# Second cross-attention of a two-layer Perceiver: scores of two key tiles, then weighted values of two key tiles

## What is computed

```python
kv = (mem @ W_kv).reshape(B, Nkv, 2, HEADS, HEAD_DIM)          # mem: (32, 1601, 256)
k = kv[:, :, 0].transpose(0, 2, 1, 3); v = kv[:, :, 1].transpose(0, 2, 1, 3)
q = (x @ W_q).reshape(B, Nq, HEADS, HEAD_DIM).transpose(0, 2, 1, 3)
attn = softmax(jnp.einsum('bhqd,bhkd->bhqk', q, k) * SCALE, axis=-1)
out = jnp.einsum('bhqk,bhkd->bhqd', attn, v).transpose(0, 2, 1, 3).reshape(B, Nq, C)
return out @ W_proj + b_proj
```

## Time and profile before

| | us |
|---|---|
| median of 3 runs | 3062.28 |
| lowest, highest | 3057.97, 3067.33 |
| profiled execution | 3058.96 |
| its span, first to last instruction | 3057.2 |
| TensorE busy in the span | 2627.0 |
| VectorE, ScalarE, GpSimd busy | 1533.6, 1410.0, 931.4 |

### The profile page before, as it was taken

How to read it: one execution, slowest core, us unless ns; L and a number is a source line. 1 busy time by engine, 2 the same in 40 slices (tenths; PEclk the granted TensorE clock), 3 DMA queues, 4 the chain that set the end, 5 groups by cost and what they waited for, 6 DMA issues and landing times.

```text
span 3057.2 us, 75335 instructions
## 1 busy us (share of the span) xinstructions
PE 2627.0 (86%) x31984; PEld 2205.9 (72%) x31988; DVE 1533.6 (50%) x2629; ACT 1410.0 (46%) x2563; POOL 931.4 (30%) x867
## 2 busy tenths in 40 slices
PE   6999732239999999999999999999999974699997
PEld 3555411138888888888888888888888753699997
DVE  3444377724445355454454454454454434477775
ACT  1221111124655655655655655655656521365564
POOL 1000034243432442442443443443443302211121
PEclk9999955569999999999999999999999975799999
DMA  8888500031110100100100100101101002466664
GB/s 340 317 319 316 212 0 0 0 119 34 35 34 23 37 31 23 45 23 23 45 23 23 45 23 29 40 23 34 34 23 34 2 1 90 156 209 202 217 200 150
DMA packets 48580, 270.17 MB, mean 88 GB/s; under 512 B 4896, under 2 KB 23584, under 8 KB 33696
## 3 DMA queue, kind: packets, MB, share of 16 engines
q1 hardware_dynamic: 40160, 255.82, 22.9%
q0 software_dynamic: 8160, 10.29, 2.2%
HBM read 247.58 MB, written 20.61 MB: 88 GB/s over the span
## 4 chain that ended last, share of the span: by engine, by line
issue 38%; PE 28%; POOL 21%; DVE 6%; DMA 3%; ACT 2%; POOLq 1%; SPq 0%; DVEq 0%; ACTq 0%
POOL k_lo L530 7%; POOL ctx_lo L538 6%; PE PS L1025 3%; PE PS L1005 3%; PE PS L1355 2%; PE PS L1356 2%; PE PS L1357 2%; POOL sideB L558 2%; POOL qbd_lo L543 2%; PE PS L1277 1%; DMA unit_raw<-in_experts 1%; PE PS L1372 1%; PE PS L1373 1%; PE PS L1374 1%; POOL slots_d L633 1%
## 5 line engine op out<-in xcount | busy, mean ns | idle before, releaser
L1624 DVE TENSOR_REDUCE mpart<-PS 128x1 f32<-128x802 f32 (+1 forms) x512 | 487.6, 987 | 464.4 <-PE PS L1141 464.4
L825 ACT ACTIVATE probs<-PS 128x1024 f32<-128x1024 f32 (+1 forms) x416 | 425.6, 1024 | 252.7 <-PE PS L1277 247.0
L530 POOL TENSOR_TENSOR k_lo<-sideB,k_hi 128x400 fp32r<-128x400 f32 (+1 forms) x256 | 255.7, 999 | 376.3 <-ACT k_hi L761 375.9
L538 POOL TENSOR_TENSOR ctx_lo<-ctx_raw,ctx_hi 128x801 fp32r<-128x801 f32 x128 | 224.6, 1764 | 459.2 <-ACT ctx_hi L773 459.2
L1277 PE MATMUL PS<-qbd_hi,k_hi 64*128 64x256 f32 (+1 forms) x1664 | 312.6, 372 | 0.0
L1141 PE MATMUL PS<-k_hi,qbd_hi 128*128 128x512 f32 (+2 forms) x1024 | 262.3, 358 | 23.1 <-POOL ctx_lo L538 13.6
L1153 PE MATMUL PS<-probs,vals 128*32 128x64 f32 x13312 | 272.9, 222 | 3.3 <-ACT probs L825 2.9
L1153 PEld LDWEIGHTS PS<-probs,vals 128*32 128x32 f32 x13312 | 205.3, 110 | 66.8 <-issue 11.0
L760 ACT COPY sideB<-PS 128x400 f32<-128x400 f32 (+1 forms) x256 | 126.6, 494 | 274.7 <-PE PS L1121 274.7
L1128 PE MATMUL PS<-wkv_hi,ctx_hi 128*128 128x256 f32 (+1 forms) x832 | 236.4, 284 | 0.0
L1277 PE MATMUL PS<-qbd_hi,k_lo 64*128 64x256 f32 (+1 forms) x1664 | 234.4, 278 | 0.1
(11 more groups left out here) (319 smaller groups left out, 6220.6 us busy)
## 6 DMA issues: line engine op xcount, KB each, us to landing
unit_raw<-in_experts SPq DMA_DIRECT2D x46, 1536.0 KB, 7.1
ctxN<-in_ctxN SPq DMA_DIRECT2D x16, 3328.0 KB, 10.8
ctxT<-in_ctxT SPq DMA_DIRECT2D x16, 3204.0 KB, 10.5
ctx_raw<-in_ctxT SPq DMA_DIRECT2D x64, 801.0 KB, 4.4
slots_d<-pad_rows SPq DMA_DIRECT2D x2, 2990.0 KB, 18.5
xg<-slots_d SPq DMA_DIRECT2D x23, 260.0 KB, 2.8
x<-in_x SPq DMA_DIRECT2D x1, 2048.0 KB, 10.0
sum_d<-x SPq DMA_DIRECT2D x1, 2048.0 KB, 6.3
```

The costliest lines, as they stand in the source:

```text
L530: g.tensor_tensor(k_lo[:, n, a, c:c + width], k_raw[p % 2][:, 0:width], k_hi[:, n, a, c:c + width].bitcast(F32), ALU.subtract).then_inc(s. ...
L538: g.tensor_tensor(ctx_lo[:, a, cols], ctx_raw[:, cols], ctx_hi[:, a, cols].bitcast(F32), ALU.subtract).then_inc(s.ctx_lo_ready, 1)
L825: act.activation(probs[rows, t % PROBS, :], PS[rows, 1024 * (t % 2):1024 * (t % 2) + 1024], ACT.Exp).then_inc(s.pr_ready, 1)
L1624: v.tensor_reduce(mpart[:, pair, half:half + 1], PS[:, at:at + width], AX, ALU.max).then_inc(s.mx_red, 1)
```

## The change

The score loop of `pe_batch` runs over pairs of key tiles. For an even t it issues the scores of t and t + 1, then finish and prepare of t, then the weighted values of t - 2 and t - 1, then finish and prepare of t + 1. Key tile 12 stands alone in its pair. Since the two weigh calls come later, each key tile's scores now wait for themselves until ScalarE has read the banks that they overwrite, that is for the exponentials of t - 2. `probs` gets a fourth buffer. Room for it comes from three places: `inv_sb` is gone (the reciprocal is written to its place in `attn4`, and multiplied there), `attn4` becomes part of `sideB`, and `attn_ch` moves behind the area that the stages share. The programs of ScalarE, VectorE and GpSimd keep their order.

```diff
-PROBS = 3
+PROBS = 4
...
-        inv_sb = sb_b("inv", [P, D])
-        attn4 = sb_b("attn4", [P, 4, P])
...
+        attn4 = sideB[:, 1792:2304].rearrange("p (g t) -> p g t", g=4)
...
-                for t in range(KEY_TILES):
+                def scores(t):
                     rows = slice(0, keys_of(t))
                     keys = slice(t * P, t * P + keys_of(t))
                     halves = [(r, slice(64 * r, 64 * r + 64)) for r in range(2)]
+                    if t >= 2:
+                        pe.wait_ge(s.pr_ready, exps_before + t - 1)
...
                     mm.then_inc(s.sc_ps, 1)
-                    if t >= 1:
-                        weigh(n, t - 1)
+
+                def beside(t):
                     if not first:
                         finish(n * KEY_TILES + t)
                     if not last:
                         prepare(n * KEY_TILES + t)
+
+                exps_before = T["pr"].now()
+                for t in range(0, KEY_TILES, 2):
+                    for one in range(t, min(t + 2, KEY_TILES)):
+                        scores(one)
+                    beside(t)
+                    if t:
+                        weigh(n, t - 2)
+                        weigh(n, t - 1)
+                    if t + 1 < KEY_TILES:
+                        beside(t + 1)
...
-                v.reciprocal(inv_sb[:, :], bank(7, D)).then_inc(s.vec_step, 1)
-                v.wait_ge(s.vec_step, own())
-                v.tensor_tensor(attn4[:, :, b * S:b * S + S], sums_sb[:, :].rearrange("p (g q) -> p g q", g=4),
-                                inv_sb[:, :].rearrange("p (g q) -> p g q", g=4), ALU.mult).then_inc(s.attn_ready, 1)
+                mine = attn4[:, :, b * S:b * S + S]
+                v.reciprocal(mine, bank(7, D).rearrange("p (g q) -> p g q", g=4)).then_inc(s.vec_step, 1)
+                v.wait_ge(s.vec_step, own())
+                v.tensor_tensor(mine, sums_sb[:, :].rearrange("p (g q) -> p g q", g=4), mine, ALU.mult).then_inc(s.attn_ready, 1)
```

More of the change, by code:

```diff
@@ L146, in build @@
         cat = sb("cat", [P, D])
-        attn_ch = sb("attn_ch", [P, KT, P])
         shift = sb("shift", [P, HEADS * S // 2], BF16)
@@ L221, in build @@
         hq_buf = sb("hq_buf", [P, 2048])
+        attn_ch = sb("attn_ch", [P, KT, P])
         identb = sb("identb", [P, P], BF16)
```

## The result

The changed kernel took 3081.62 us (median of 4 runs, 3080.72 to 3087.41) against 3060.34 us for the kernel before in the same comparison. The ratio is 1.007, with a 95% interval of 1.0048 to 1.0091: **slower by about 21 us**. The forecast was 3032 us, faster, and its range ended at 3052. The profiled execution of after has a span of 3079.8 us, that of before 3057.2.

The account below looks back on a forecast made before the run. TensorE was taken to bound stage B. Joints -42.2, step 2 wait +18.8, step 4 -5.3, GpSimd ahead +1.7 and first pair +0.5 gave -26.5 us from 3058.96: 3032 us forecast, range 3016 to 3052.

Parts of the forecast that it names:

- The joints: Stage B, TensorE: joining same-shape groups saves 0.09 us per score pair and 0.13 per weighted-values pair, -42.2 us in all.
- The rivals in which the joints give nothing or only half: Stage B: joints worth nothing, 3072 us, chance 0.07; only weighted values join, 3050 us, chance 0.13 including partial joints.
- The wait at step 2: TensorE's transposes wait 1.34 us for the normalised tile in 15 pairs, +18.8 us, bounds 0 and 20.
- The same instructions of the same size: Fourth buffer, moved tiles and reciprocal written in place cost nothing, on VectorE while TensorE projects.
- the paragraph on ScalarE: Exponentials cause no wait in plain key tiles; only the first pair, without finish steps, meets ScalarE, +0.5 us.
- The clock: Rival: granted clock falls after step 2's wait, three key tiles at half clock, 54 us, 3085 us; chance 0.04.
- Step 4: TensorE's wait for spread keys falls from 0.62 to about 0.3 us, -5.3 us over 15 pairs, bounds 0 and -8.
- GpSimd ahead of the next batch (n = 1): Before the next batch's first maxima, the 0.13 us wait stays or grows by up to 0.1; +1.7 us taken.
- The first pair: Without finish steps, its scores start back to back and meet ScalarE and its rounding: +0.5 us.

Follow-up runs that it names:

- the runs with 1.27 and 1.56: Changed kernel, GpSimd's first context subtraction held until the normalised tile is written: 3039.65 us; kernel before, context rounded one key tile earlier: 3080.63 us.
- the kernel with single tiles and GpSimd's wait: Changed kernel with old order for key tiles 0 to 3 where n = 0, and GpSimd's first context subtraction held until the normalised tile: 3027.99 us.
- the kernel in which GpSimd waits: Changed kernel, but GpSimd begins its first context subtraction in a pair only when VectorE has written the normalised tile: 3039.65 us, ratio 0.9933.
- the kernel of single tiles: Changed kernel with old order for key tiles 0 to 3 where n = 0 and finish steps exist, pairs from tile 4: 3033.52 us, ratio 0.9911.

## Why the prediction was wrong, step by step

**The joints: right.** Forecast 0.09 us per joined score pair and 0.13 per joined weighted values. Measured 0.09 (0.12 instead of 0.21 at the joint) and 0.15 (1.03 instead of 1.18). With n = 1, where nothing disturbs it, the part with scores fell from 25.31 to 23.93 us, 1.38 us for six joints of each kind; the forecast was 6 x 0.22 = 1.32. The rivals in which the joints give nothing or only half are refuted.

**The wait at step 2: this step failed.** The sum took a chain "at a fixed distance" of 3.31 us behind step 0, which gave 1.34 us of wait, "bounds 0 and 20" us in all. The chain was not fixed: its last instruction depends on what GpSimd is doing when it starts. With the lock the wait is 2.80 us. The term is not +18.8 but 14 x 2.78 + 1.1 = 40 us, outside its bounds. Where GpSimd is held back, the wait is 1.27 us and the term is right. The prediction looked at GpSimd in this chain only for the reciprocal root that feeds the normalisation. It did not ask which instruction GpSimd has next, when that becomes ready, and whether the change moves that. "The same instructions of the same size" was true, and "cost nothing" was not: the paragraph on ScalarE saw that ScalarE gets its work earlier, but not what that releases. The clue stood in before's trace: GpSimd's 1503.60 is 0.15 us behind VectorE's 1503.45 and waits 0.18 us for ScalarE.

**The clock: the mechanism right, its chance and its size wrong.** The rival stood at 0.04 and 54 us. What it says did happen, at 11 of 14 waits. Its price was too high (three key tiles at half clock each; measured are 3.4 or 6.8 us of half clock, much of it over projections, and about 1.6 us lost per pair, 22 us in all). That its 3085 us lies near the measured 3081.6 is luck: it had 54 us for the clock and nothing for the lock, which took about 22 us each. Its chance was set by one wait of 1.72 us without a fall. That was evidence for a wait of 1.3 us, as the runs with 1.27 and 1.56 confirm, but not for 2.8 (and at that same early place a wait of 2.08 us did bring a fall, in the kernel with single tiles and GpSimd's wait, at 731.6): the argument stood on the size of the wait, and fell with it.

**Step 4: right.** Forecast about 0.3 us of wait left; measured 0.3 in 14 places where GpSimd waits, and at most 0.3 in after.

**GpSimd ahead of the next batch (n = 1): too high.** In the kernel in which GpSimd waits, the last weighted values start at 1573.37 and the maxima at 1574.56, 1.19 us later; two groups take 1.03 to 1.05, so 0.14 to 0.16 us are left, against 0.13 before. The term is some +0.4, not +1.7.

**The first pair: wrong.** It was to gain 2 x 1.32 less 0.5 us, that is 2.1. Up to the first step 0 the kernel with GpSimd's wait takes 1.0 us more than before (818.1 against 817.1), after 4.3, with a fall of the clock in it. Without finish steps the scores wait for ScalarE; this is PE in the kernel with GpSimd's wait:

```profile
730.48 0.39 PE L1276 MATMUL PS<-shift,onesb 64*128 64x512 bf16 x2 [1.65 <-ACT probs L826]
...
738.90 0.53 PE L1142 MATMUL PS<-k_hi,qbd_hi 128*128 128x512 f32 x2 [1.22 <-issue]
```

The first row is the wait of the earlier trace rows in a new place. The second is new, and the profile names nothing that ended it. The 0.5 us stood for the first kind only.

**Without the lock the sum is off by 7 of its 26.5 us.** Where GpSimd waits, the time is 3039.65 against the forecast 3032.5. The 7 us lie as follows, by spans against before. Up to the first step 0: forecast -2.1, measured +1.0. The 14 distances: forecast 14 x (-2.64 + 1.25 - 0.35 + 0.11) = -22.8, measured 1570.5 - 1590.4 = -20.0 (the difference of the unrounded sums); most of it is that an undisturbed pair gives 1.5 and not 1.63. Behind them: forecast -1.6, measured -0.6 (4.9 gained up to the last step 0, 4.2 lost behind it, 564.95 against 560.71). TensorE's products are the same there. In before the clock is at its lower level for 131 us of it, in the kernel with GpSimd's wait for 155; the table by stretch has it in its mean:

```profile
2496.48:3057.19 560.71, 458.64 (x3602) 445.61 (x3602) 339.18 (x486) 260.49 (x357) 116.65 (x92) 0.88 0.52 167
2472.60:3037.55 564.95, 464.77 (x3602) 450.21 (x3602) 339.16 (x486) 259.95 (x357) 116.64 (x92) 0.86 0.52 166
```

The nine profiled executions agree: the five with 129 to 134 us at the lower level take 557.4 to 560.7 us for this part, the one with 141 takes 563.9, the three with 154 or 155 take 564.2 to 567.3. No experiment shows what sets the length of the low stretch.

## What to carry to other kernels

When a change shifts when an engine gets its data, look not only at the chain that the critical engine waits for, but at what else the same event releases on the engines that share something with it: here one instruction released both VectorE's last step and GpSimd's next, and 0.07 us decided who went first and 1.54 us were lost, 14 times. Where two such instructions are released together, set the order by a wait, which costs nothing on the engine that has time. And a wait of the engine that bounds the kernel has to be priced with what follows it: up to 1.56 us these waits at step 2 cost their own length, at 1.97 us and more the clock came on top, though not each time.

## What the runs showed of the hardware

- **A lock, not a slowdown.** VectorE's normalisation (128x256, one input from memory and two scalars) took 0.41 us alone, 1.95 when a GpSimd subtraction of 1.87 us had begun 0.07 us before it, and 1.11 when that subtraction was cut in two. It ends 0.15 us after the GpSimd instruction in front of it (1520.44 to 1520.59; the same with halves), so some 0.26 us of its own 0.41 go by in the wait, as the profile has it. The other way round GpSimd pays: two subtractions take 3.90 us in before, the first starting while the normalisation runs, and 3.74 us when they start behind it.
- **Short waits of TensorE can lower its clock.** At step 2, waits of 1.27 and 1.56 us never did (14 each), waits of 1.97 us did in 5 of 14 cases, of 2.63 and 2.80 us in 11 of 14 each. The falls lasted 3.4 or 6.8 us. Nor is the length all: in the first pair of after a wait of 1.48 us (741.84), 8.7 us behind one of 1.63 (733.17), was followed by a fall, and so was a stop of 1.57 us at 1794.28 in the kernel of single tiles, while 1.72 us at 732.39 in before was not. What decides in a single case is open.
- **A joint is free when the shape stays.** From scores to scores 0.12 us pass, from scores to weighted values 0.21, also when the second score group has its own semaphore wait in front of it.
